# A pipelined graph-network kernel: the tasks outside the loop in another order on four engines

## What is computed

```python
mask = (adj > 0.0).astype(x.dtype)
W1a, W1b = (W1[:F], W1[F:])
xj_proj = x @ W1a
diff = x[:, :, None, :] - x[:, None, :, :]
h = jax.nn.relu(xj_proj[:, :, None, :] + diff @ W1b + b1)
hm = jnp.einsum('bjkh,bjk->bjh', h, mask)
deg = jnp.sum(mask, axis=-1)
x = _layernorm(x + hm @ W2 + deg[..., None] * b2, axis=-1)
```

## Time and profile before

| what | value |
|---|---|
| median of three runs | 252.81 us |
| the profiled execution's own time | 252.74 us |
| its span in the profile | 250.9 us |
| TensorE busy | 235.9 us, 94% |
| VectorE busy | 226.6 us, 90% |
| ScalarE busy | 209.8 us, 84% |
| GpSimd busy | 121.4 us, 48% |
| transfers | 18.20 MB, mean 73 GB/s |

### The profile page before, as it was taken

How to read it: one execution, slowest core, us unless ns; L and a number is a source line. 1 busy time by engine, 2 the same in 40 slices (tenths; PEclk the granted TensorE clock), 3 DMA queues, 4 the chain that set the end, 5 groups by cost and what they waited for, 6 DMA issues and landing times. The chain is left out here.

```text
span 250.9 us, 9244 instructions
## 1 busy us (share of the span) xinstructions
PE 235.9 (94%) x2810; PEld 188.7 (75%) x2813; DVE 226.6 (90%) x778; ACT 209.8 (84%) x572; POOL 121.4 (48%) x288
## 2 busy tenths in 40 slices
PE   7947989999999999999999999999999999998992
PEld 2524758888787878787888878887878888886761
DVE  4757699999999999999999999999999999997763
ACT  2384888989998989899899999898999989987631
POOL 1124444363645637463736364563736483576225
PEclk9985899999999999999999999999999999999998
DMA  6983003221212213131313021221310110000002
GB/s 201 357 325 106 3 4 123 70 84 30 70 54 78 73 55 96 44 107 42 106 39 107 14 74 59 64 82 47 105 44 25 43 46 0 25 24 1 3 8 63
DMA packets 10550, 18.20 MB, mean 73 GB/s; under 512 B 1296, under 2 KB 7696, under 8 KB 10512
## 3 DMA queue, kind: packets, MB, share of 16 engines
q1 hardware_dynamic: 10512, 17.73, 21.7%
HBM read 15.63 MB, written 2.10 MB: 71 GB/s over the span
## 5 line engine op out<-in xcount | busy, mean ns | idle before, releaser
L1327 PE MATMUL ring<-hot,vh 128*128 128x128 bf16 (+9 forms) x768 | 117.4, 255 | 1.3 <-ACT ring L914 1.0
L1327 PE MATMUL ring<-hot,vl 128*128 128x128 bf16 (+9 forms) x768 | 116.3, 251 | 0.0
L1796 DVE SCALAR_TENSOR_TENSOR sums<-ring,sums 128x256 f32<-128x256 f32 (+10 forms) x240 | 97.8, 428 | 4.3 <-PE ring L1327 1.9
L1327 PEld LDWEIGHTS ring<-hot,vh 128*128 128x128 f16 (+1 forms) x768 | 62.0, 104 | 23.6 <-issue 16.8
L1327 PEld LDWEIGHTS ring<-hot,vl 128*128 128x128 f16 (+1 forms) x768 | 61.9, 103 | 2.4
L661 POOL TENSOR_TENSOR vl<-vf,vh 128x384 f16<-128x384 f32 x32 | 29.7, 929 | 63.2 <-ACT vf L870 59.4
L903 ACT COPY ring<-u_sb 128x192 f32<-128x192 f32 (+8 forms) x160 | 49.3, 359 | 7.4 <-DVE sums L1796 7.4
L900 ACT COPY ring<-u_sb 128x512 f32<-128x512 f32 (+1 forms) x80 | 43.3, 559 | 0.4 <-issue 0.2
L715 POOL TENSOR_TENSOR sums<-taken,sums 128x512 f32<-128x512 f32 x16 | 20.7, 1292 | 27.1 <-ACT taken L932 27.1
L821 ACT CAST maskT<-bx 128x512 bf16<-128x512 f32 x32 | 18.5, 586 | 14.3 <-PE bx L1171 13.8
L1771 DVE TENSOR_SCALAR hot<-slotT 128x944 bf16<-128x944 f16 (+6 forms) x112 | 28.6, 280 | 0.0
(11 more groups left out here) (119 smaller groups left out, 463.7 us busy)
## 6 DMA issues: line engine op xcount, KB each, us to landing
adj_sb<-adj SPq DMA_DIRECT2D x16, 512.0 KB, 3.7
x_sb<-x_pairs SPq DMA_DIRECT2D x16, 128.0 KB, 2.3
xT_sb<-xT SPq DMA_DIRECT2D x16, 128.0 KB, 2.1
x_all<-x SPq DMA_DIRECT2D x4, 512.0 KB, 7.9
out<-o_sb SPq DMA_DIRECT2D x16, 128.0 KB, 1.7
wts<-weights SPq DMA_DIRECT2D x1, 417.0 KB, 4.8
cst_general<-general SPq DMA_DIRECT2D x1, 256.0 KB, 3.2
cst_half<-half SPq DMA_DIRECT2D x1, 137.0 KB, 3.1
```

Source lines behind the costliest of these rows:

```text
L1327: return eng.matmul(to if part == "main" else to[g * HT:g * HT + HT], values, selection, start=False, stop=final, skip_group_check=True)
L1796: eng.scalar_tensor_tensor(out=to, in0=view(pair, part, unit, piece), scalar=0.0, in1=to, op0=ALU.max, op1=ALU.add).then_inc(added[part], 1)
```

## The change

Only the two lists of calls outside `body` change, on TensorE, VectorE, ScalarE and GpSimd. No step is added or removed and none has other work; only the place in the queue differs. SyncE's list is the same. The diff, cut to what the prediction speaks of (VectorE's list stands last):

```diff
             widen_ident()
             degrees(Pair(0, 0))
             corrections(Pair(0, 0))
+            degree_bias(Pair(0, 0))
             add_weights()
-            degree_bias(Pair(0, 0))
-            residual(Pair(0, 0))
+            degrees(Pair(0, 1))
             low_v(Pair(0, 0), 0)
             low_v(Pair(0, 0), 1)
-            degrees(Pair(0, 1))
-            scale_outputs(0)
+            scale_inputs()
+            scale_outputs(1)
             corrections(Pair(0, 1))
-            scale_inputs()
-            degree_bias(Pair(0, 1))
+            degrees(Pair(0, 2))
+            residual(Pair(0, 0))
             add_taken(Pair(0, 0), 0)
             low_v(Pair(0, 1), 0)
-            degrees(Pair(0, 2))
+            corrections(Pair(0, 2))
             low_v(Pair(0, 1), 1)
-            scale_outputs(1)
-            corrections(Pair(0, 2))
+            degree_bias(Pair(0, 1))
+            scale_outputs(0)
             run(eng, body)
...
             seed_joint(Pair(0, 14))
-            seed(Pair(0, 15), "tail", 0)
-            seed(Pair(0, 15), "tail", 1)
+            copy_permT(Pair(0, 15))
             seed(Pair(0, 15), "main", 0)
             clamp_small(Pair(0, 14))
-            copy_permT(Pair(0, 15))
-            deviation(Pair(0, 13))
+            seed(Pair(0, 15), "tail", 1)
             take_out(Pair(0, 15), 0)
             seed(Pair(0, 15), "main", 1)
             seed(Pair(0, 15), "main", 2)
...
             gather(Pair(0, 14), "tail", 3)
+            add_over()
+            gather(Pair(0, 15), "main", 0)
             gather(Pair(0, 15), "tail", 0)
             gather(Pair(0, 15), "tail", 1)
-            gather(Pair(0, 15), "main", 0)
-            keep_busy_last(7)
             gather(Pair(0, 15), "main", 1)
...
             unsort_y(Pair(0, 14))
-            add_over()
             project(Pair(0, 15))
+            unsort_y(Pair(0, 15))
+            keep_busy_last(7)
             keep_busy_last(2)
-            unsort_y(Pair(0, 15))
...
             sort_key(Pair(0, 0))
+            make_ident()
             ranks(Pair(0, 0))
             permutation(Pair(0, 0))
+            masks(Pair(0, 1))
+            prepare_weights()
             ranks_above(Pair(0, 0))
-            prepare_weights()
-            masks(Pair(0, 1))
+            count_given(Pair(0, 0))
+            weight_top()
+            masks(Pair(0, 2))
+            first_max()
             count_masks(Pair(0, 1))
-            count_given(Pair(0, 0))
-            count_least(Pair(0, 1))
-            first_max()
-            weight_top()
             first_scales()
-            masks(Pair(0, 2))
             select(Pair(0, 0), 0)
```

More of the change, by code:

```diff
@@ L1032, in _ @@
             copy_slots(Pair(0, 14), 1)
+            copy_u_main(Pair(0, 14))
+            take_out(Pair(0, 13), 0)
             seed(Pair(0, 13), "main", 1)
-            take_out(Pair(0, 13), 0)
+            seed(Pair(0, 13), "main", 2)
             copy_u_tail(Pair(0, 14))
-            seed(Pair(0, 13), "main", 2)
-            copy_u_main(Pair(0, 14))
             copy_y(Pair(0, 12))
-            seed(Pair(0, 13), "tail", 2)
             seed(Pair(0, 13), "main", 3)
@@ L1043, in _ @@
             deviation(Pair(0, 11))
+            seed(Pair(0, 13), "tail", 2)
             seed(Pair(0, 13), "main", 4)
             full_v(Pair(0, 14), 1)
-            seed(Pair(0, 14), "tail", 0)
             high_v(Pair(0, 14), 1)
             seed(Pair(0, 13), "main", 5)
+            seed(Pair(0, 14), "tail", 0)
             copy_maskT(Pair(0, 15), 0)
@@ L1051, in _ @@
             seed_joint(Pair(0, 13))
-            copy_permT(Pair(0, 14))
+            seed(Pair(0, 14), "tail", 1)
             copy_slots(Pair(0, 15), 0)
-            seed(Pair(0, 14), "tail", 1)
+            copy_slots(Pair(0, 15), 1)
             clamp_small(Pair(0, 13))
             copy_xs(Pair(0, 15))
-            copy_slots(Pair(0, 15), 1)
             seed(Pair(0, 14), "main", 0)
+            copy_permT(Pair(0, 14))
             seed(Pair(0, 14), "main", 1)
+            take_out(Pair(0, 14), 0)
             copy_u_main(Pair(0, 15))
-            take_out(Pair(0, 14), 0)
-            deviation(Pair(0, 12))
             seed(Pair(0, 14), "main", 2)
@@ L1083, in _ @@
             seed(Pair(0, 15), "main", 2)
+            sum_over()
+            deviation(Pair(0, 13))
+            seed(Pair(0, 15), "tail", 2)
             seed(Pair(0, 15), "main", 3)
             seed(Pair(0, 15), "main", 4)
-            seed(Pair(0, 15), "tail", 2)
             seed(Pair(0, 15), "main", 5)
+            seed_joint(Pair(0, 15))
             copy_y(Pair(0, 14))
-            seed_joint(Pair(0, 15))
             clamp_small(Pair(0, 15))
-            sum_over()
             copy_y(Pair(0, 15))
@@ L1448, in _ @@
             sort_x(Pair(0, 0))
+            excess_tail(Pair(0, 0))
+            number_slots(Pair(0, 0), 1)
+            excess_main(Pair(0, 0))
             keep_busy(1)
-            number_slots(Pair(0, 0), 1)
-            excess_tail(Pair(0, 0))
             add_first_up()
             keep_busy(3)
-            set_banks(0)
-            excess_main(Pair(0, 0))
             hidden_u_main(Pair(0, 0))
@@ L1459, in _ @@
             hidden_v(Pair(0, 0))
+            set_banks(0)
             set_banks(1)
@@ L1498, in _ @@
             gather(Pair(0, 1), "main", 1)
+            hidden_v(Pair(0, 2))
             gather(Pair(0, 1), "main", 2)
-            hidden_v(Pair(0, 2))
             unsort_y(Pair(0, 0))
@@ L1968, in _ @@
             most()
+            count_least(Pair(0, 1))
             select(Pair(0, 0), 3)
@@ L1971, in _ @@
             scales()
+            scale_down(0)
             count_rest(Pair(0, 1))
             select(Pair(0, 0), 5)
-            scale_down(0)
-            make_ident()
             run(eng, body)
+            add(Pair(0, 12), "main", 2)
+            sort_key(Pair(0, 14))
             select(Pair(0, 13), 6)
-            sort_key(Pair(0, 14))
-            add(Pair(0, 12), "main", 2)
             add_residual(Pair(0, 11))
@@ L2029, in _ @@
             add(Pair(0, 13), "main", 4)
+            select(Pair(0, 14), 8)
+            ranks_above(Pair(0, 15))
+            add(Pair(0, 13), "main", 7)
             add(Pair(0, 13), "tail", 7)
-            add(Pair(0, 13), "main", 7)
+            add(Pair(0, 13), "tail", 5)
             select(Pair(0, 14), 9)
-            ranks_above(Pair(0, 15))
-            add(Pair(0, 13), "tail", 5)
+            add(Pair(0, 13), "tail", 6)
+            inverse_deviation(Pair(0, 11))
             select(Pair(0, 14), 10)
             count_given(Pair(0, 15))
-            inverse_deviation(Pair(0, 11))
-            add(Pair(0, 13), "tail", 6)
             add(Pair(0, 13), "main", 5)
@@ L2102, in _ @@
             add_residual(Pair(0, 15))
+            statistics(Pair(0, 15))
             inverse_deviation(Pair(0, 14))
-            statistics(Pair(0, 15))
             last_mean()
```

125 lines of the change are left out of this document (63 added, 62 removed).

## The result

The changed kernel takes 258.58 us (median of four executions, 256.25 to 260.24); the kernel before, beside it, 253.03 us (four, 252.63 to 254.0). The ratio is **1.0183, 95% interval 1.0106 to 1.0259**: slower by 1.8%, more than twice the forecast +1.8 us. The medians differ by 5.55 us, and 258.58 lies outside the range (253.4 to 256.6). The profiled execution is the 256.25 us one, the shortest of the four: its span is 254.4 us against 250.9 before, and its mean granted clock 0.966 against 0.977. The other three had clocks of 0.950 to 0.951 and spans of 256.6 to 258.4 us. So the trace shows 3.5 us of the loss, of an execution that lies inside the range; the other 2 us are in executions without a trace. Ratios here leave out executions over 1.5% above the fastest of their kernel: one of the four here, and half of those of `fill` and `tail_only`.

The account below looks back on a forecast made before the run. A latency chain at the start, then TensorE almost without idle time and VectorE full from pair 1's selection. Start +2.5 and end -0.7 gave +1.8 us on 252.74: 254.6 us, range 253.4 to 256.6.

Parts of the forecast that it names:

- The transfer holds `masks(2)`: VectorE, start: moved ahead, masks(2) still waits for adj and starts at 17.20 us, after 5 us of waiting.
- rival 4: Start: the transfer isn't what holds masks(2), or adj(2) lands before 12 us; no start cost, 252.0 us; 4%.
- w1abs in 0.35 us: VectorE, start: w1abs takes 0.35 us instead of 0.88, as GpSimd has nothing to do there.
- u and v at half clock: TensorE, pair 0: u starts at 20.4 us, its two steps take about 2.1 us; hidden_v at 23.3 instead of 19.48.
- The clock returns at about 24 us: TensorE, start: unbroken work raises the clock, hidden_v ends at 24.6, fills take 0.9 us, keys(1) starts at 25.5 (+3.3).
- Behind `start_sums(0)` full clock, ScalarE back to back: Before pair 1's selection: ScalarE's copies run without waits, slots at 32.0 us instead of 29.50; start costs +2.5 us.
- rival 1: Start: the clock stays low, costing 0.9 to 1.8 us more, 255.5 to 256.4 us; 21%.
- The loop keeps the loss: Loop: VectorE is full from pair 1's selection in both kernels, so the start's 2.5 us stay.
- Rival 2: Tail, ScalarE 230.2 to 233.5 us: gives back what the start takes, -1.8 us; 252.8 to 253.5 us; 17%.
- Rival 3: Second low_v(1) on GpSimd: corrections(2) slips over 0.6 us, TensorE waits before pair 1's first gather; 255.1 to 257; 8%.
- The end, -0.7: Tail, pair 15: take_out, add_taken and main 3's gather come earlier; -0.7 us, between -0.2 and -1.8.
- +2.8 on VectorE: VectorE, start: work behind the transfer makes pair 0's selection start at about 20.6 us instead of 17.81.

Follow-up runs that it names:

- fill: Changed kernel with keep_busy(8) before add_weights_up and keep_busy(20) for keep_busy(1) before add_first_up; median 257.01 us of four, no ratio.
- tail_only: Kernel before's lists ahead of the loop, the changed kernel's behind it; ratio 0.9959, ten executions from 251.09 to 255.52 us, median 254.63.
- after_again: The changed kernel's text measured once more, against the kernel before; 259.3 us, profiled execution 258.86, ratio 1.0228.
- hold: Changed kernel with fillers wherever TensorE waits at the start, so the clock is held, VectorE's order untouched; 253.68 us, ratio 1.0035.
- held_head: Kernel before, old tail, with fillers at the start that hold the clock; median 250.77 us, ratio 0.9927.
- masks2_back: Changed kernel with the one line masks(2) moved back behind first_scales on VectorE; 254.35 us, ratio 1.0047.
- held_back: Changed kernel with masks(2) moved back behind first_scales and fillers at the start holding the clock; median 250.52 us, ratio 0.9908.

## Why the prediction was wrong

The verdict, slower, had 75% and came; the size did not. Point by point:

- **The transfer holds `masks(2)`**: right. 5.60 us of waiting; rival 4 is out. The 17.20 was taken as fixed; it came at 17.58, and 17.00 to 18.13 in the other traces (+0.38).
- **w1abs in 0.35 us**: right to the digit, and the selection of pair 0 came 20.89 - 17.58 = 3.31 behind the start of `masks(2)`, where 3.4 stood.
- **u and v at half clock**: right. u's two steps took 2.37 us (20.80 to 23.17), 2.1 forecast, so that term was 0.3 too small; `hidden_v(0)` began at 23.89 (23.3, with 0.38 of the difference from the transfer). The prediction missed that `masks(1)` now stands ahead of `prepare_weights`: TensorE waits 1.79 us for w_abs at 11.00. The clock fell at 12.6 behind it in this execution. In after_again, with 1.99 us of the same wait, it fell at 17.0, and the first mark is the same (16.75), so the early fall costs nothing here.
- **The clock returns at about 24 us**: this step failed. It returned at 26.2, `hidden_v(0)` took 1.65 instead of some 1.3, the fills 1.40 instead of 0.9, and `keys(1)` began at 26.71 instead of 25.5. Of the 1.21 us 0.38 are the transfer's, 0.2 those of u's steps and 0.62 the late return's. The prediction named "27 us" as a sign that it is wrong, and 26.71 comes close to that.
- **Behind `start_sums(0)` full clock, ScalarE back to back**: this failed too. It was named as a possibility ("down again in the 1.5 us that TensorE waits for `permutation(1)`") and put at the edge of rival 1. The clock fell at 29.7, right behind the waits of 1.44 and 0.55 us. From the second maskT to the selection it took 4.50 us instead of 3.45; in hold, with the clock up, it took 3.46, so the term itself was right and the clock in it wrong. The sum of the misses at the second maskT (29.78 for 28.55: 0.38 and 0.85) and behind it (1.05) is the 2.28 between 34.28 and 32.0.
- **Rival 1 (the clock stays low, +0.9 to +1.8, 21%)** was the case, at its upper end (+1.9 at the first mark) in the shortest execution; the other executions are longer still. The traced 256.25 us lie in rival 1's 255.5 to 256.4 and inside the range, which ended at 256.6; the median lies outside it. The mechanism that failed thus accounts for the traced miss (+1.65 us on 254.6). The 2.3 us more in the median had no term in the sum, and no trace of such an execution exists but after_again's, which has them at the end. The range should have gone on: the moment of the clock's return was taken as one value, and the change made two falls out of one.
- **The loop keeps the loss**: right. Between the second and third mark nothing is given back but the 0.55 us of the tail's lists.
- **Rival 2** (the tail gives back what the start takes) did not come. **Rival 3** did not either: `corrections(2)` did wait 3.62 us on GpSimd, the second `low_v(1)` ran at 44.30, and the distance to the joint seed is not longer for it.
- **The end, -0.7**: right, step by step, in the profiled execution (20.59 against 21.29). In after_again it was +1.6 instead (22.88): the late store and a fall of the clock ahead of the last steps stood in no term. From the joint seed, take_out 2.61 us later (2.69 forecast), `add_taken` done after 4.56 (4.59), the gather of main 3 after 6.19 (6.19). Ahead of the joint seed the lists gave 0.5 us more that had not been counted.

There is a second reading of the failed step. The sum took the old start, 12.33, as a base at which the clock cost nothing. It cost 12.33 - 10.66 = 1.67 us there too. Measured at full clock the change of order costs 13.80 - 10.66 = 3.14; the low clock adds 2.90 in the new order (16.70 - 13.80) and 1.67 in the old; 3.14 + 2.90 - 1.67 = 4.37. The prediction's +2.8 on VectorE was near the first term. It added 0.5 us up to `keys(1)` and took 0.8 off behind it, for a clock that would be better than before there, when it was worse.

**What stays open.** Why the last store lands late in three of fourteen traces; all three have the new tail, but seven others with it don't, and the old tail has only four traces, in which other stores of `out` landed late. And the three executions of the changed kernel that took 2 to 4 us more than the profiled one beside it have no trace; their mean clocks (0.950 and 0.951) are lower, but where it was low isn't known. The one traced execution of that length, after_again's, has the loss at its end and a mean clock of 0.965. Whether the new tail makes such ends more frequent, as half of tail_only's executions suggest, no run here settles.

## What to carry to other kernels

A step that waits for a transfer and is moved ahead of other work costs not its wait (5.60 us here) but the work that used to run under that wait and now stands behind it (3.17 us at full clock), and that on every engine that this work feeds; here one line (`masks(2)`) of the whole diff made some four fifths of the loss. Where TensorE is at the end of such a chain of latencies, look at the granted clock first in the old kernel: filling its waits with matmuls into an unused bank (15 more of them in held_head, with the two `set_banks` moved into the waits) gave 0.7% to the old kernel and, with more of them, 1.5 to 2% to the changed one, more than the new tail's order did. And measure a change of order with the clock held in both versions, since the clock's luck was larger than most of the parts to be told apart.

## What the runs showed of the hardware

- The granted clock falls and returns at different moments of the same program: in two traces of the changed kernel it fell at 12.6 and at 17.0 us, and returned at 26.2 and at 27.3. That the return differs from run to run of the same kernel is what the Trainium skill says ("TensorE: Matmul & The Clock Gate", part 1); the two traces agree. In the changed kernel it also fell at 29.7 us, behind waits of only 1.44 and 0.55 us, and not when those waits were filled (hold).
- w1abs took 0.88 us beside GpSimd's `xb` and 0.35 in the kernels whose GpSimd had nothing to do there, masks2_back and held_back among them, where it stands at its old place in time (14.32 and 14.69 us). In masks2_back a `ranks_above` of 64 columns, 0.23 us elsewhere, took 0.97 beside GpSimd's `low_v` (timelines of VectorE and GpSimd):

```profile
23.88 0.97 DVE L1658 TENSOR_TENSOR above<-rank,cst_single 128x64 bf16<-128x64 f32 x1
...
23.86 0.91 POOL L661 TENSOR_TENSOR vl<-vf,vh 128x384 f16<-128x384 f32 x1 [0.57 <-ACT vf L870]
```

  VectorE's operation ends 0.08 us behind GpSimd's, which began 0.02 us earlier. GpSimd's two operations kept their usual time (0.73 and 0.91 us), so VectorE's are the ones that waited. The page "SBUF — State Buffer" of the Trainium skill ("Who interferes with whom") says that a VectorE operation in a two-port mode, which a TENSOR_SCALAR such as w1abs can enter, and a GpSimd one hold the shared ports for a whole instruction, and that a VectorE operation with two inputs in SBUF contends with a GpSimd one that reads SBUF. The trace agrees with both; which of the two issued first can't be read, since their records begin within 0.02 us of each other.
- The last store, 128 KB, lands 1.7 us after its issue in eleven traces and 3.3 to 3.6 us in three. As the last transfer of the kernel it is nowhere hidden. Earlier stores of the same size landed after up to 3.2 us in the kernel before and 3.3 in hold.
